# Causal masks written by TensorE under the logits, other banks and another order of work in an attention and FFN block

## The chip, the cores and the metric

One core of a Trainium2 chip. The metric is the device time of one execution in microseconds; three runs of the kernel before have a median of 406.66 us (405.45 to 406.77). TensorE multiplies, VectorE, ScalarE and GpSimd (POOL in the rows) do elementwise work, SyncE issues most DMAs. PSUM has eight banks, all in use.

## The reference

Eight sequences of 512 tokens with 128 channels pass through causal attention with 16 heads of 8 channels, a layernorm, a gated FFN on a time-shifted mixture, and a second layernorm:

```python
qkv = x @ w_attn + b_attn                      # x: (8, 512, 128)
att = softmax(where(causal, (q @ k.T) / sqrt(8), -inf))
y   = (att @ v) @ w_proj + b_proj
x1  = layernorm(x + y)
xr, xk = mu_r*x1 + (1-mu_r)*x1_prev, mu_k*x1 + (1-mu_k)*x1_prev
out = layernorm(x1 + sigmoid(xr @ W_r.T) * (square(relu(xk @ W_k.T)) @ W_v.T))
```

All is float32 at the borders. The kernel keeps q and k as sums of three bf16 parts (high, mid, low).

## The kernel before

A batch (one sequence) has 4 groups of 10 units, so 40 steps, and 8 batches make 320 steps. A unit is one 128x512 bank of logits at most: one half (side) of the array's rows, and one or two 64-row tiles of the triangle, as `EX_TILES` lists them; two heads stand in the two halves of the columns (`ab`). Every logit is computed twice. `maxima(m)` (L407 to L423) computes q·k into a bank of `mx_ps` for the row maxima: `reduce_maxima` (L681) on VectorE adds a mask and reduces with one instruction and an accumulator read for each tile. The maxima of a group are split into two bf16 parts by POOL (`parts`, L902), turned by VectorE (`maxima_turned`) and put by four DMAs of SyncE (`stack_maxima`, L304) into rows of `q_st`, where they act as one more term of the product. `logits(n)` (L425 to L440) then computes k·q minus the maximum, transposed, into a bank of `ex_ps`, ScalarE takes the exponential into `probs` (`exps`, L592), POOL sets the triangle behind the diagonal to zero with affine selects (`zero_behind`, L917; the waits of their users go through `squares_zeroed`), and `weighted_values` (L442 to L457) multiplies with the values in float32, which also gives the row sums.

Maxima run 20 steps ahead (`LEAD`), changed by `AHEAD` at some steps. Since there are two banks for logits, `logits(n)` waits until the exponential n-2 is done; the three maxima banks work likewise. In step 20 of a batch the maxima of the next batch begin, and these need the next batch's stacked q and k: xT is transposed (step 2), q (step 6) and k (step 7) are multiplied, ScalarE rounds the high part (`highs`, L597), VectorE takes the rest (`rests`, L705), ScalarE the mid part (`mids`, L603), POOL the low part (`lows`, L944), and SyncE copies each part into its bands of `q_st` or `k_st` with twelve DMAs of 128 KB (`stack`, L284, issue at L295), in one queue with `stack_maxima`, loads and stores.

Stage products (xT, q, k, v, proj, x1T, kT, r, kv) share two banks `sh_ps`, dealt in turn (`shared_uses`, L81). After the attention of a batch, during the next one, VectorE turns the sums (`sums_turned`, L713), divides (`normalise`, L718), turns again, adds the residual, takes statistics and aggregates (L737, L744); POOL forms rstd (`deviations`, L955); VectorE norms (`attention_normed`, L757); TensorE, ScalarE and POOL do the FFN.

Each engine has its queue, written out by hand: in step n every engine runs its step's unit and then the stage work that the tables `PE_AT`, `ACT_AT`, `DVE_AT`, `POOL_AT` put at that step (a number over 40 is a step of the next batch, a negative one a step of the batch before). All engines run in order, so a wait holds all that stands behind it. Before the loop stands a head for batch 0; behind it a tail that does the last batch's stages in halves.

## Time and profile before

| | |
|---|---|
| median of three runs | 406.66 us |
| the profiled execution | 407.86 us, span 406.1 us |
| busy: PE | 330.0 us, 81% |
| busy: DVE | 287.2 us, 71% |
| busy: ACT | 208.9 us, 51% |
| busy: POOL | 205.9 us, 51% |
| mean granted clock of TensorE | 0.812 |

### The profile page before, as it was taken

The page shows a single profiled execution, that of the slowest core. Times are in us where ns is not written, and L with a number is a line of the kernel's source. Part 1 is how long each engine was busy: PE and PEld are TensorE (multiplying, and loading weights), DVE is VectorE, ACT ScalarE, POOL GpSimd, SP SyncE. Part 2 cuts the span into 40 slices and gives each one's busy share as a digit, 9 for nine tenths or more (in the row PEclk, how much of TensorE's full clock was granted, in tenths as well). Part 3 has the DMA queues.
Part 4 walks back from the last instruction along what each step waited for, and adds up shares of the span by engine and source line. Part 5 has one row for each costly group of instructions (what it writes and reads, how often), then busy time and mean ns, then how long its engine had stood idle before and what let it go on. Part 6 is the DMA issues. An engine that isn't in the chain of part 4 may idle for free.

```text
span 406.1 us, 10267 instructions
## 1 busy us (share of the span) xinstructions
PE 330.0 (81%) x3721; PEld 153.5 (38%) x3721; DVE 287.2 (71%) x1326; ACT 208.9 (51%) x405; POOL 205.9 (51%) x404
## 2 busy tenths in 40 slices
PE   5268778987989698978998698979897989796853
PEld 2123323333443335333533335343534354424442
DVE  3379757788676887697778886887789778922254
ACT  3204655674565545583557546654667465544211
POOL 8131533453353933567454833593358545944642
PEclk9756758597979979796969888986999698669678
DMA  2611411041101410052102310141105100000000
GB/s 57 177 35 30 133 33 51 6 115 46 54 2 45 129 49 21 6 133 78 29 5 78 108 54 1 44 131 46 29 6 148 38 27 2 21 11 1 2 26 26
DMA packets 33114, 20.65 MB, mean 51 GB/s; under 512 B 7400, under 2 KB 33064, under 8 KB 33064
## 3 DMA queue, kind: packets, MB, share of 16 engines
q1 hardware_dynamic: 33064, 20.00, 18.3%
q8 instruction: 29, 0.48, 0.5%
q14 instruction: 21, 0.17, 0.1%
HBM read 4.72 MB, written 2.10 MB: 17 GB/s over the span
## 4 chain that ended last, share of the span: by engine, by line
PE 55%; DVE 16%; SPq 10%; ACT 5%; issue 5%; DMA 4%; POOL 4%; POOLq 0%; DVEq 0%; ACTq 0%
PE pv_ps L453 20%; PE ex_ps L437 12%; DVE masked L691 10%; SPq L295 7%; PE mx_ps L420 6%; ACT probs L592 5%; PE sh_ps L381 3%; SPq L304 3%; DMA q_st<-q_part 2%; PE sh_ps L494 2%; POOL probs L917 2%; PE sh_ps L391 2%; PE sh_ps L471 2%; PE sh_ps L463 2%; PE sh_ps L395 2%
## 5 line engine op out<-in xcount | busy, mean ns | idle before, releaser
L691 DVE CUSTOM_DVE_ANT_0 masked<-mx_ps,mask_wide 128x448 f32<-128x448 f32 (+7 forms) x512 | 204.9, 449 | 64.1 <-PE mx_ps L420 59.2
L592 ACT ACTIVATE probs<-ex_ps 128x512 f32<-128x512 f32 (+1 forms) x320 | 164.3, 553 | 145.1 <-PE ex_ps L437 142.7
L917 POOL TENSOR_SCALAR_AFFINE_SELECT probs<-probs 64x192 f32<-64x192 f32 (+2 forms) x212 | 94.9, 462 | 122.6 <-ACT probs L592 117.7
L420 PE MATMUL mx_ps<-k_st,q_st 64*64 64x128 bf16 (+7 forms) x1024 | 122.2, 346 | 29.2 <-DVE m_max L691 14.3
L437 PE MATMUL ex_ps<-q_st,k_st 64*64 64x64 bf16 (+7 forms) x1024 | 121.3, 340 | 21.9 <-ACT probs L592 18.9
L453 PE MATMUL pv_ps<-probs,vals 128*32 128x512 f32 (+7 forms) x1024 | 92.7, 489 | 0.0
L437 PEld LDWEIGHTS ex_ps<-q_st,k_st 64*64 64x64 bf16 x1024 | 44.4, 116 | 109.5 <-ACT probs L592 80.4
L420 PEld LDWEIGHTS mx_ps<-k_st,q_st 64*64 64x64 bf16 x1024 | 45.2, 117 | 55.1 <-DVE m_max L691 29.9
L691 DVE DVE_READ_ACCUMULATOR2_ANT m_max<- 128x1 f32 x512 | 42.5, 83 | 0.0
L453 PEld LDWEIGHTS pv_ps<-probs,vals 128*32 128x32 f32 x1024 | 26.4, 120 | 36.0 <-issue 27.5
L977 POOL TENSOR_SCALAR o_sb<-h,mv,rstd 128x128 f32<-128x128 f32 x28 | 22.1, 801 | 1.2 <-POOL rstd L960 1.1
L966 POOL TENSOR_TENSOR kact<-relu 128x512 f32<-128x512 f32 x7 | 7.3, 1039 | 20.2 <-ACT relu L627 15.8
L960 POOL TENSOR_TENSOR rstd<-var_eps,exponent 128x4 f32<-128x4 f32 x14 | 14.5, 1039 | 1.2
L737 DVE BATCH_NORM_STATS2 stats<-h 128x6 f32<-128x128 f32 x56 | 13.3, 281 | 2.2 <-POOL h L971 2.1
L761 DVE TENSOR_SCALAR x<-h,mv,rstd 128x128 f32<-128x128 f32 x28 | 7.9, 346 | 8.2 <-POOL rstd L960 8.2
L381 PE MATMUL sh_ps<-ident,x_in 128*128 128x128 f32 x32 | 7.8, 393 | 5.4 <-DMA x_in<-in_L_attn_x_dram 3.8
L716 DVE STREAM_TRANSPOSE y_rows<-pv_ps 128x512 f32<-128x512 f32 x15 | 10.7, 712 | 2.0 <-PE pv_ps L453 2.0
L907 POOL CAST m_part<-m_max 128x16 bf16<-128x16 f32 x32 | 6.3, 196 | 10.9 <-DVE m_max L691 9.0
L463 PE MATMUL sh_ps<-w_o,ynT 128*128 128x128 f32 x56 | 9.9, 332 | 2.2 <-DVE ynT L733 2.2
L494 PE MATMUL sh_ps<-w_mix,kact 128*128 128x128 f32 x56 | 10.8, 353 | 0.0
L476 PE MATMUL sh_ps<-w_mix,x1T 128*128 128x128 f32 x56 | 10.8, 275 | 0.0
L475 PE MATMUL sh_ps<-w_mix,x1T 128*128 128x128 f32 x56 | 10.8, 275 | 0.0
(126 smaller groups left out, 319.1 us busy)
## 6 DMA issues: line engine op xcount, KB each, us to landing
q_st<-q_part SPq DMA_DIRECT2D x48, 128.0 KB
k_st<-k_part SPq DMA_DIRECT2D x48, 128.0 KB, 2.4
x_in<-in_L_attn_x_dram SPq DMA_DIRECT2D x8, 256.0 KB, 2.8
q_st<-m_turn SPq DMA_DIRECT2D x128, 2.0 KB
x_res<-in_L_attn_x_dram SPq DMA_DIRECT2D x8, 256.0 KB, 2.7
out_dram<-o_sb SPq DMA_DIRECT2D x7, 256.0 KB, 2.3
q_st<-zero_b SPq DMA_DIRECT2D x8, 32.0 KB
out_dram<-o_sb SPq DMA_DIRECT2D x2, 128.0 KB, 1.8
```

The costliest lines, as they stand in the source:

```text
L295: sp.dma_start(st[band::BANDS, :, :], part_of[:, part, :]).then_inc(sem_of, 16)
L381: last = pe.transpose(ps[:, t * P:(t + 1) * P], src(t), ident[:, :])
L420: last = mm(ps[half_rows(ab), at:at + n], q_st[par][side_rows(s), slot, i * BLK:(i + 1) * BLK], k_st[par][side_rows(s), slot, 0:n], start= ...
L437: last = mm(ps[half_rows(ab), at:at + w], k_st[par][side_rows(s), slot, j * BLK:(j + 1) * BLK], q_st[par][side_rows(s), slot, j * BLK:T], ...
L453: last = mm(pv_ps[c * VW:(c + 1) * VW, j * BLK:T], vals[b % 2][:, 2 * c + h, j, :], probs[B % 2][:, gp, at:at + T - j * BLK], start=i == 0 ...
L463: last = mm(ps[:, t * P:(t + 1) * P], ynT[:, t * P:(t + 1) * P], w_o[:, :], start=True, stop=True)
L494: last = mm(ps[:, t * P:(t + 1) * P], kact[:, t * P:(t + 1) * P], w_mix[:, 4, :], start=True, stop=True)
L592: act.activation(probs[B % 2][:, gp, u * T:u * T + w], ex_bank(n)[0][:, 0:w], ACT.Exp, scale=SCALE).then_inc(exp_done, 1)
L691: last = dve.tensor_tensor_reduce(out=masked[m % len(masked)][:, at:at + n], in0=mx_ps[m % MX_BANKS][:, at:at + n], in1=mask_wide[:, T - n ...
L917: pool.affine_select(out=squares, in_=squares, compare_op=ALU.is_ge, fill=0.0, base=0, pattern=[[0, count], [1, BLK]], channel_multiplier= ...
L960: pool.tensor_tensor(rstd[i][:, :], var_eps[i][:, :], exponent[:, :], ALU.pow).then_inc(rstd_ready[i], 1)
L977: pool.tensor_scalar(o_sb[:, t, :], h2[:, t, :], mv[1][:, t, 0:1], rstd[1][:, t:t + 1], ALU.subtract, ALU.mult).then_inc(o_done, 1)
```

## The change

TensorE writes the masks: ahead of the logits of a unit, two matmuls of an identity (`ident_b`) with a triangle of large negative numbers (`behind_b`) go into the diagonal squares of the bank, and the logits are added to them. POOL's selects, `squares_zeroed` and the semaphore `causal` are gone; `weighted_values` waits for the exponentials. The tiles of a unit are in another order, so that both diagonal squares can be addressed by one pattern.

`ex_ps` has three banks and `sh_ps` one. For batch 0 each stage product has a bank of its own among banks not yet in use.

Small work is dealt out anew. ScalarE writes, besides the high part, a full copy of q and k (`q_full`, `k_full`), and POOL takes the rest from these two. POOL multiplies by the reciprocal sums (`normalise`), VectorE only takes the reciprocals (`shares`). The aggregates are gone for all batches but the last: POOL's `deviations` works from the statistics of even and odd columns with seven small operations in place of two, and gives a shift as well; ScalarE norms with scale and bias.

All tables are new, and a second set of them (`PE_END`, `ACT_END`, `DVE_END`, `POOL_END`, `PV_END`, `PV_LAST`) holds for stage work of the last batches. `AHEAD` now holds maxima back by one or two steps in steps 18 to 27.

In the head the weights and half of the bias go out on ScalarE's queue, and so do k's six stacking DMAs of batch 0; x is transposed in two halves that ScalarE and VectorE copy; VectorE takes the mid parts of batch 0; `b_v_wide` and its wait for the small vectors stand behind six maxima; and TensorE runs 5, 2 and 16 products of zeros (`idle_products`) between the head's work.

The diff, cut to its core:

```diff
-EX_TILES = ((0,), (1, 7), (2, 6), (3, 5), (4,))
+EX_TILES = ((0,), (7, 1), (6, 2), (5, 3), (4,))
-MX_BANKS, EX_BANKS = 3, 2
-AHEAD = {0: 0, 32: 1, 33: 1, 34: 3, 35: 3, 36: -1}
-PV_AT = {4: (0, 1), 6: (2, 3), 8: (4, 5), 10: (6, 7)}
-PE_AT = {"xT": -38, "q": -34, "k": -33, "v": -25, "proj": 59, "x1T": 69, "kT": 72, "r": 72, "kv": 78}
+MX_BANKS, EX_BANKS = 3, 3
+IDLE = (5, 2, 16)
+WT_AT = 8
+AHEAD = {2: 1, 8: 2, 9: 2, 13: 1, 18: -1, 19: -2, 20: -2, 21: -2, 22: -1, 23: -1, 24: -2, 25: -2, 26: -2, 27: -2,
+         36: 1, 37: 2, 38: 2, 39: -1}
+PV_AT = {0: (0,), 5: (1,), 7: (2, 3, 4), 8: (5,), 11: (6, 7)}
+PE_AT = {"xT": -40, "q": -37, "k": -35, "v": -25, "proj": 57, "x1T": 68, "kT": 74, "r": 76, "kv": 78}
+ACT_AT = {"xT": -40, "q": -37, "k": -35, "q_mid": -32, "k_mid": -31, "v": -25, "norm1": 67, "norm1b": 67, "x1T": 68,
+          "kT": 73, "r": 76}
+POOL_AT = {"q_rest": -35, "k_rest": -33, "q_low": -29, "k_low": -28, "yn0": 33, "yn1": 54, "residual": 6,
+           "deviations1": 64, "squares": 71, "add2": 81, "deviations2": 95, "norm2": 98}
+PE_END = {"proj": 59, "x1T": 70, "kT": 72, "r": 75, "kv": 77}
...
         ex_ps = [bank_of(f"ex_ps{i}") for i in range(EX_BANKS)]
-        sh_ps = [bank_of(f"sh_ps{i}") for i in range(2)]
+        sh_ps = bank_of("sh_ps")
+        head_ps = dict(zip(AHEAD_OF_ALL, (sh_ps, mx_ps[1], ex_ps[0], ex_ps[1], pv_ps, ex_ps[2], sh_ps)))
...
             sp.dma_start(x_in[0][:, :, :], x_d[0]).then_inc(xin_loaded[0], 16)
-            sp.dma_start(w_in[:, :], w_attn).then_inc(w_in_loaded, 16)
...
             for part in range(3):
-                for which in range(2):
-                    stack(which, part, 0)
+                stack(sp, 0, part, 0)
...
                 (ps, before), at = ex_bank(n), 0
                 wait(pe, exp_done, n - before + 1)
+                hidden = behind_b[side_rows(s), 0:2, :] if len(tiles) > 1 else behind_b[side_rows(s), 0, :]
+                for ab in range(2):
+                    mm(diagonals(ps, ab, T - tiles[0] * BLK, len(tiles)), ident_b[side_rows(s), :], hidden,
+                       start=True, stop=False, skip_group_check=True)
...
-                                  q_st[par][side_rows(s), slot, j * BLK:T], start=True, stop=True)
+                                  q_st[par][side_rows(s), slot, j * BLK:T], start=False, stop=True,
+                                  skip_group_check=True)
...
-                wait(pe, causal, squares_zeroed(2 * B + groups[-1], k, j))
+                wait(pe, exp_done, (2 * B + groups[-1]) * UNITS + SIDES * (k + 1))
...
+            def idle_products(n, bank_of_idle):
+                for _ in range(n):
+                    mm(bank_of_idle[:, :], idle[:, 0:P], idle[:, :], start=True, stop=True)
...
+            idle_products(IDLE[2], mx_ps[0])
             pe.wait_ge(ones_stacked[0], 16)
-            for m in range(MX_BANKS):
+            for m in range(WT_AT):
                 maxima(m)
...
                 act.activation(part[:, 0, :], ps[:, :], ACT.Identity, bias=bias[:, 0:1]).then_inc(high[i], 1)
+                if b > 0:
+                    act.activation(full[:, :], ps[:, :], ACT.Identity, bias=bias[:, 0:1]).then_inc(read, 1)
...
+            def attention_normed(b, tiles):
+                wait(act, h2_done, b)
+                wait(act, shift_ready[0], b + 1)
+                for t in tiles:
+                    act.activation(x1[:, t, :], h1[:, t, :], ACT.Identity, scale=rstd[0][:, t:t + 1],
+                                   bias=shift[0][:, t:t + 1]).then_inc(x1_done, 1)
...
+            act.dma_start(w_in[:, :], w_attn).then_inc(w_in_loaded, 16)
+            load_bias(act, 1, b_k)
...
+            for part in range(3):
+                stack(act, 1, part, 0)
...
+                if m == WT_AT - 2:
+                    dve.wait_ge(vecs_loaded, 64)
+                    dve.tensor_copy(b_v_wide[:, :], b_v[:, 0:1].to_broadcast([P, P])).then_inc(consts_v, 1)
...
-            def zero_behind(G, ab, first, apart, count):
...
-            def group_zeroed(G, second):
...
-            def unit_zeroed(G, k):
...
+            def rests(i, b):
+                full, part, rest = ((q_full, q_part, q_rest), (k_full, k_part, k_rest))[i]
+                wait(pool, high[i], b + 1)
+                wait_read(pool, ("q", "k")[i], b)
+                pool.tensor_tensor(rest[:, :], full[:, :], part[:, 0, :], ALU.subtract).then_inc(rested[i], 1)

```

## Rows read from the trace of the kernel before

**Rows 1.** Chain of waits of the page, share of the span by engine

```profile
PE 55%; DVE 16%; SPq 10%; ACT 5%; issue 5%; DMA 4%; POOL 4%; POOLq 0%; DVEq 0%; ACTq 0%
```

**Rows 2.** Windows: stretch, length, busy of PE, PEld, DVE, ACT, POOL; clock, DMA

```profile
35.07:73.93 38.86, 31.17 (x366) 12.52 (x362) 28.45 (x140) 24.22 (x47) 13.69 (x30) 0.68 0.22 58
...
73.93:337.57 263.64, 230.37 (x2788) 107.31 (x2784) 205.47 (x971) 154.40 (x300) 140.51 (x263) 0.86 0.21 55
...
295.13:337.57 42.44, 36.97 (x468) 17.67 (x468) 34.75 (x165) 25.62 (x51) 24.38 (x45) 0.89 0.20 53
337.57:379.71 42.14, 34.64 (x360) 15.98 (x364) 21.76 (x97) 22.04 (x43) 27.25 (x65) 0.78 0.03 9
```

**Rows 3.** Windows around the clock: before a fall, after it, and a full-speed stretch

```profile
93.00:96.40 3.40, 1.79 (x12) 1.18 (x12) 2.65 (x12) 1.28 (x3) 2.34 (x6) 1.00 0.30 78
96.40:103.30 6.90, 6.60 (x56) 2.08 (x59) 4.50 (x25) 2.17 (x4) 2.17 (x5) 0.51 0.11 24
...
280.80:314.90 34.10, 29.31 (x414) 14.88 (x406) 29.04 (x137) 22.75 (x45) 18.79 (x34) 1.00 0.21 57
```

**Rows 4.** TensorE's matmul waits, 73.93 to 337.57: total us, times, longest

```profile
PE ex_ps L437 <- ACT probs L592: 12.0, 32, 0.8
PE mx_ps L420 <- DVE m_max L691: 10.3, 18, 0.8
PE mx_ps L420 <- DMA q_st<-q_part: 4.3, 3, 1.6
```

**Rows 5.** Timeline of SyncE's queue and TensorE in batch 4: start, us, what [idle]

```profile
217.40 1.88 SPq L295 DMA_DIRECT2D q_st<-q_part  x3
...
227.15 0.58 SPq L295 DMA_DIRECT2D q_st<-q_part  x1
...
230.25 0.65 PE L420 MATMUL mx_ps<-k_st,q_st 64*64 64x512 bf16 x4 [1.55 <-DMA q_st<-q_part]
```

**Rows 6.** Groups by line, engine, tiles and form: busy us, mean ns, idle

```profile
L917 POOL TENSOR_SCALAR_AFFINE_SELECT probs<-probs 64x192 f32<-64x192 f32 (+2 forms) x212 | 94.9, 462 | 122.6 <-ACT probs L592 117.7
...
L947 POOL TENSOR_TENSOR q_part<-q_rest,q_part 128x512 bf16<-128x512 f32 x7 | 8.1, 1157 | 0.0
...
L761 DVE TENSOR_SCALAR x<-h,mv,rstd 128x128 f32<-128x128 f32 x28 | 7.9, 346 | 8.2 <-POOL rstd L960 8.2
...
L723 DVE TENSOR_TENSOR yn_rows<-y_rows,rden 128x256 f32<-128x256 f32 x15 | 6.4, 425 | 0.5
...
L710 DVE SCALAR_TENSOR_TENSOR q_rest<-sh_ps,b_q,q_part 128x512 f32<-128x512 f32 x8 | 6.0, 748 | 3.9 <-ACT q_part L601 3.9
...
L601 ACT ACTIVATE q_part<-sh_ps,b_q 128x512 bf16<-128x512 f32 x8 | 5.5, 683 | 2.3 <-PE sh_ps L391 2.3
```

**Rows 7.** Timeline of TensorE: matmuls of 64 and 128 columns, full, then half clock

```profile
221.28 0.19 PE L437 MATMUL ex_ps<-q_st,k_st 64*64 64x64 bf16 x2
221.74 0.22 PE L437 MATMUL ex_ps<-q_st,k_st 64*64 64x128 bf16 x2
...
47.50 0.32 PE L437 MATMUL ex_ps<-q_st,k_st 64*64 64x128 bf16 x2
```

**Rows 8.** Timelines: the head (four engines), then one stage product and its reader

```profile
15.66 0.61 SPq L295 DMA_DIRECT2D k_st<-k_part  x1
...
18.17 1.06 PE L420 MATMUL mx_ps<-k_st,q_st 64*64 64x512 bf16 x8 [6.83 <-DMA k_st<-k_part]
...
22.71 0.23 DVE L790 COPY b_v_wide<-b_v 128x128 f32<-128x128 f32 x1 [8.21 <-DMA mu<-in_L_ffn_mu_k_dram]
...
35.07 0.60 ACT L592 ACTIVATE probs<-ex_ps 128x512 f32<-128x512 f32 x1 [13.69 <-PE ex_ps L437]
...
214.69 1.13 PE L391 MATMUL sh_ps<-xT,w_q 128*128 128x512 f32 x2
...
216.69 0.68 ACT L601 ACTIVATE q_part<-sh_ps,b_q 128x512 bf16<-128x512 f32 x1
```

**Rows 9.** Timeline of VectorE near the end of batch 7

```profile
366.35 1.19 DVE L761 TENSOR_SCALAR x<-h,mv,rstd 128x128 f32<-128x128 f32 x4 [8.25 <-POOL rstd L960]
```

More of the change, by code:

```diff
@@ new lines, with due @@
+PV_LAST = {22: (0,), 23: (1, 2), 24: (3, 4, 5), 27: (6, 7)}
+TABLES = {"PE": (PE_AT, PE_END), "ACT": (ACT_AT, ACT_END), "DVE": (DVE_AT, DVE_END), "POOL": (POOL_AT, POOL_END)}
+GROUP_AT = {"parts": 1, "turn": 2}
+SHARED = tuple(PE_AT)
+AHEAD_OF_ALL = ("xT", "xT2", "q", "k", "v", "wT", "bp")
+def due(engine, name, n):
+    at, end = TABLES[engine]
+    last = NB - 2 if at[name] > STEPS else NB - 1
+    if name in end and n == last * STEPS + end[name]:
+        return last
+    s, rest = divmod(n - at[name], STEPS)
+    first, last = (0, last - 1) if name in end else (1, last)
@@ L96, in shared_uses @@
             if s is not None:
[L97 to L101 removed]
+                at[s, name] = len(at) + 1
+    return at
+SHARED_USES = shared_uses()
 def wait(eng, sem, value):
@@ L278, in in_bank, with load_bias, stack @@
             return slice(t * P % HALF, t * P % HALF + P)
+        def load_bias(eng, i, bias):
+            natural = b_attn[i * C:(i + 1) * C].rearrange("(s j d a) -> s d j a", s=SIDES, d=HD, a=1)
+            for s in range(SIDES):
+                eng.dma_start(bias[side_rows(s), :], natural[s],
+                              allow_slow_non_contiguous=True).then_inc(b_qk_loaded, 16)
+        def stack(eng, which, part, b):
+            par = b % 2
+            if part == 0:
+                wait(eng, exp_done, (b - 1) * STEPS)
+                if which == 0 and b > 0:
+                    eng.dma_start(q_st[par][MAX_BAND::MAX_STEP, :, :], zero_b[:, :]).then_inc(q_stacked, 16)
+            st, part_of, sem_of = ((q_st[par], q_part, q_stacked), (k_st[par], k_part, k_stacked))[which]
+            wait(eng, (high, mid, low)[part][which], b + 1)
+            for band, band_part in enumerate((Q_PARTS, K_PARTS)[which]):
+                if band_part == part:
+                    eng.dma_start(st[band::BANDS, :, :], part_of[:, part, :]).then_inc(sem_of, 16)
         block = ctx.enter_context(nc.Block())
@@ L781, in _ @@
                                 ).then_inc(consts_v, 1)
+            ps, read = wait_full(dve, "xT2", 0)
+            dve.tensor_copy(xT[:, HALF:T], ps[:, 0:HALF]).then_inc(read, 1)
             dve.wait_ge(b_qk_loaded, 64)
-            rests(0, 0)
-            rests(1, 0)
-            for i, (part, rest) in enumerate(((q_part, q_rest), (k_part, k_rest))):
-                dve.wait_ge(mid[i], 1)
-                dve.tensor_tensor(part[:, 2, :], rest[:, :], part[:, 1, :], ALU.subtract).then_inc(low[i], 1)
+            for i in range(2):
+                first_rests(i)
+                first_mids(i)
+            for i in range(2):
+                first_lows(i)
+            for half in range(2):
+                last = dve.tensor_copy(ident_b[half_rows(half), :], ident[half_rows(half), half * BLK:(half + 1) * BLK])
+            last.then_inc(consts_v, 1)
+            dve.wait_ge(mask_ready, 6)
+            dve.tensor_copy(behind_b[:, :, :], behind[:, :, :]).then_inc(consts_v, 1)
             dve.memset(q_st[1][:, :, :].bitcast(U32), 0).then_inc(consts_v, 1)
-            dve.wait_ge(vecs_loaded, 64)
-            dve.tensor_copy(b_v_wide[:, :], b_v[:, 0:1].to_broadcast([P, P])).then_inc(consts_v, 1)
-            dve.wait_ge(mask_ready, 3)
             for n in range(-LEAD, EXPS + BEHIND):
@@ L998, in _ @@
                 pool.wait_ge(mask_ready, 2 + ab)
+            pool.memset(behind[:, :, :], 0.0).then_inc(mask_ready, 1)
+            pool.wait_ge(mask_ready, 4)
+            for ab in range(2):
+                here = behind[half_rows(ab), :, :]
+                pool.affine_select(out=here, in_=here, compare_op=ALU.is_ge, fill=MASKED, base=0,
+                                   pattern=[[0, 2], [1, BLK]], channel_multiplier=-1).then_inc(mask_ready, 1)
+                pool.wait_ge(mask_ready, 5 + ab)
             pool.memset(vals[0][:, :, :, :], 0.0).then_inc(consts_g, 1)
```

399 lines of the change are left out of this document (204 added, 195 removed).

## The prediction

> **What bounds the kernel now.** I read the chain of waits first. Over half of the span passes on TensorE, a sixth on VectorE and a tenth in the queue of SyncE that issues the stacking transfers [rows 1]. So TensorE leads, and it is not alone. Next the stretches by batch: the profiled execution (span 406.13 us; 407.86 us as timed, against a median of 406.66 us) falls into a head of 35.1 us to the first exponential, batch 0 with 38.9 us, six regular batches with 263.6 us together, so 43.9 us each, batch 7 with 42.1 us, and the rest, 26.4 us [rows 2]. Of a regular batch TensorE is busy 38.4 us, VectorE 34.2, ScalarE 25.7, POOL 23.4 [rows 2]. TensorE's 38.4 busy us are not 38.4 us of full-speed work: the mean granted clock is 0.86 of full, which is about 33.0 us of work at 2.4 GHz. The period is therefore 33.0 us of work, 5.4 us lost to the clock, and 5.5 us idle.
>
> The third view is the clock around its falls. In the 3.4 us ahead of a fall TensorE was busy 1.79 us (waiting in the middle of a batch for the next batch's stacks), then it ran 6.9 us at 1.2 GHz; in the 34.1 us that passed wholly at 2.4 GHz it was busy 29.3 us [rows 3]. The Trainium skill (TensorE: Matmul & The Clock Gate, HAM oscillation) ties a return to half rate to long waits of TensorE; here its longest regular wait is about 1.6 us, and the clock falls all the same, so I go by the rows. The fourth view is what TensorE waits for in the six batches: ScalarE's release of one of two logits banks 12.0 us, VectorE's release of a maxima bank 10.3, the last part of q 4.3 [rows 4]. The weight-load row of the same answer is longer, but weight loads run beside matmuls, so I price from the matmul rows only. The fifth is the queue of SyncE: the first piece of q is issued at 217.4 us, the last at 227.15, and the maxima of the next batch start at 230.25 after a wait of 1.55 us [rows 5].
>
> **The change, part by part.**
>
> *POOL's zeroing goes.* 212 selects, 94.9 us in all, 11.9 us a batch [rows 6]. POOL is not the bound, so this pays only where somebody waited. In the regular batches that is nobody I can see in the matmul rows of [rows 4]; in the last one it is real, since the rstd of batch 6 stands behind selects that wait for exponentials, and VectorE sat idle 8.25 us for it, with TensorE behind [rows 9]. I take nothing from regular batches here and return to batch 7 below.
>
> *TensorE's triangles come.* Each of 320 steps gets two more 64-row matmuls of 64 or 128 columns ahead of the logits, on the same rows as the logits. The trace holds matmuls of this size in the same quarter of the array: one of 64 columns took 0.19 us and one of 128 took 0.22 at full clock, 0.32 at half [rows 7]. The constant part overlaps the next one, so the added time is the slope: 0.03 us for 64 columns, twice for 128, the two halves of the array side by side. A group has 4 steps of 64 and 6 of 128 columns: 4×0.03 + 6×0.06 = 0.48 us, 1.9 us a batch; with 10 per cent for issue, 2.1 us. Bounds: 0 if all of it lies in waits, and 80 whole durations of about 0.2, 16 us, if nothing overlapped; I stay at the slope since the rows of both forms show pairs starting together. The Trainium skill (same page, Back-to-back issue gap) puts an issue floor of about 25 ns under a small matmul; by it the 64-column ones would cost the same 0.03 us, and the sum would not move.
>
> *A third bank for logits, one for stages.* This takes aim at the 12.0 us of [rows 4], 2.0 us a batch. With three banks an exponential may end a step later before TensorE stands. ScalarE also gets more: one full copy each of q and k at up to 0.69 us, and four norms of 128 columns, at most half of that each, so up to 2.7 us a batch, bounded below by 1.5 when they start back to back. I take half, 1.0 us. The price is the single stage bank: nine uses a batch, each of which must be read before the next may be written. The rows show one such turn: q's product starts at 214.69, its reader runs at 216.69 for 0.68 [rows 8]. Now two reads stand there, and k's product waits for both. The tables put two to eleven steps between neighbours, so I add 0.5 us a batch, and make the dear case a rival.
>
> *VectorE's small work.* Off it go the rests of q and k (2×0.75), both products of normalise (2×0.43), four norms (1.13 a batch from 7.9 us in 7 batches), together 3.5 us, and eight small aggregates besides [rows 6]. That leaves some 30 us of 34.2. What TensorE waits for it, 10.3 us in six batches, is 1.7 a batch; I take 0.6 of that. Who waits on POOL for the same work: its rests are like the low parts, 1.16 us instead of 0.75 [rows 6], so the chain high, rest, mid, low grows by 0.8 us for the pair, and POOL has selects of 11.9 us less in its queue. The small operations of deviations go from two to seven; I bound them by nothing and by 0.4 us each and take 0.2, which lengthens the chain to the norm by 1 us; it has many steps of slack except in batch 7.
>
> *Preparation earlier, maxima later.* q's product moves from step 6 to 3 and k's from 7 to 5, and the first maxima of the next batch are let back by two steps. A step is about 1.1 us (43.9/40), so the queue of [rows 5] starts some 3 us earlier and its result is wanted 2 us later, against 1.55 us of wait and 0.8 of chain. That wait goes: 4.3 us by [rows 4] plus the start behind it, 1.0 us a batch. Issues on SyncE stay as many and in the same order, so nothing new is queued behind a wait there.
>
> *Sum of a regular batch.* Idle 5.5 − 1.0 (banks) + 0.5 (stage bank) − 0.6 (VectorE) − 1.0 (stacks) = 3.4 us. Work 33.0 + 2.1 = 35.1. With the clock at 0.86 that would be 40.8 + 3.4 = 44.2, nothing gained. But the clock fell behind lean stretches, and two of the edits fill these: no wait at the stacks, and more columns in each step. In the batch at 0.89 the period was 42.4, and that still with one slow stretch [rows 2]. I take one slow stretch less per batch, a clock of 0.95: 36.9 + 3.4 = 40.3. Gain 3.6 us, six times 21.6.
>
> *Head.* The last piece of k was issued at 15.66 and the first maxima ran from 18.17; then VectorE waited until 22.71 for vectors that it needs only for b_v_wide, and the first exponential came at 35.07 [rows 8], 12.3 us behind. Now that copy stands behind six maxima, and q and k go out on two queues. 12 issues of about 0.6 us in one queue [rows 5] become six and six; the last k is issued around 12.8, as the low parts are ready then, so maxima start at about 15.5, VectorE half a us later, and the first exponential at 16.1 + 12.1 = 28.2. Gain 6.9 us. Sixteen idle products stand ahead of the first maxima: at 2.4 GHz, 0.2 us each, they end in time; at half clock they end 2 us late. The Trainium skill (DMA: Bandwidth & Descriptors, Issuing engines are not separate DMA queues) calls what a second issuing engine saves usually small; by that the 2.7 us of it would be gone, and the head would gain 4.2.
>
> *Batch 0 and batch 7, rest.* Batch 0 has less on TensorE (31.2 us busy of 38.9) and VectorE, relieved by its share, is near its bound; with the wait for the stacks gone I take 2.5 us. Batch 7: the regular gain of 3.6 us and half of a VectorE wait that TensorE shared [rows 9] but which the longer deviations eat; 3.6 in all. The rest after the last exponential keeps its chain; without selects ahead of it 0.5 us.
>
> Total: 6.9 + 2.5 + 21.6 + 3.6 + 0.5 = 35.1, so a span of 371.0; with the 0.5 us by which the median lies over the span, 371.5.
>
> **Rivals.** *A, the clock holds all through.* The 34.1 us at full clock [rows 3] show that it can. Then 35.1 work and 14 per cent idle as in that row (4.8 of 34.1), less the 1.9 us of the edits: 35.1 + 5.7 − 1.9 = 38.9, a further 1.4 us in eight batches, and up to 2 us more in head and rest: 358. *B, the clock stays as it is.* Lean stretches come back at kT, r and kv, which remain. Then the regular batches give nothing (44.2), and head, batch 0 and rest give 9.9: 396. *C, slower: the single stage bank.* Each of nine products waits for the reader of the one before, at the head of TensorE's queue, with all logits and maxima behind it. My gains are 35 us over 63 such turns, so it decides from 35/63 = 0.56 us of wait per turn; the row of q shows 1.3 us from product to end of one reader [rows 8], and at 0.8 us a turn it costs 50 us: 421. Against it: the tables leave steps in between. *D, the triangles aren't hidden and cost like whole small matmuls* on the logits path, 0.2 us in 40 steps, 8 us a batch where I took 2.1: eight batches add 47 us to 371.5, 418; against it speak the pairs that start together.
>
> **Chances.** Forecast 0.60 (about 363 to 383), A 0.18, B 0.13, C 0.05, D 0.04. The likeliest is 371.5. The range takes in A with a few us below it, and leaves out C, D and most of B, 2 in 10 together: 353 to 391. A measurement tells about 0.3 per cent, 1.2 us, from no change. Faster 0.90, the same 0.02 (B with a worse head), slower 0.08.
>
> **What would show it.** First exponential at 28 us; nine turns without waits over 0.5 us on the stage bank; no TensorE wait for the last part of q; logits waits for ScalarE halved; granted clock in regular batches 0.95 and period 40.3; VectorE busy 30 us a batch. Wrong would be: a clock of 0.86 with a busier TensorE (B), stage products idle before (C), matmuls of the triangles with 0.1 us or more of their own (D).

## The result, and the profile after

The kernel after takes 335.69 us (333.71 to 336.87), the one before 406.06 (405.23 to 406.77), four runs each: a ratio of 0.826 [0.821, 0.831]. That is faster, as forecast, and by twice the forecast: 70 us in place of 35, below the whole range. Here and below every median takes in all executions, and the ratios leave out the few that came out in a slower state. The profiled execution of after has a span of 331.8 us and a mean granted clock of 0.950 (406.1 and 0.812 before).

The page of after: instructions busy, the granted clock in 40 slices (tenths), the chain of waits. To be read against the table of before and [rows 1].

```profile
PE 295.2 (89%) x4384; PEld 155.4 (47%) x4384; DVE 262.3 (79%) x1220; ACT 218.3 (66%) x445; POOL 145.0 (44%) x310
...
PEclk9965879899999999999999999999999999999958
...
PE 58%; DVE 13%; ACT 8%; POOL 7%; issue 6%; SPq 4%; DMA 2%; ACTq 0%; POOLq 0%; DVEq 0%
```

In the clock's line a 9 stands for 90 per cent of full speed or more. TensorE is now busy 89 per cent of the span; SyncE's queue, 10 per cent of the chain before, is 4. From the ninth slice (66 us) to the 38th the clock never falls. The stretches, with the same columns as [rows 2]: head, batch 0, the first regular batch alone, all six of them, batch 7, the rest.

```profile
0.00:32.36 32.36, 24.14 (x138) 9.55 (x138) 23.25 (x81) 4.71 (x7) 15.76 (x35) 0.79 0.41 93
32.36:65.02 32.66, 27.52 (x446) 14.30 (x448) 26.26 (x136) 24.51 (x49) 7.49 (x13) 0.87 0.26 69
65.02:101.15 36.13, 34.58 (x548) 17.96 (x544) 30.55 (x148) 27.41 (x57) 12.88 (x26) 0.98 0.24 63
65.02:276.31 211.29, 202.51 (x3268) 107.47 (x3264) 183.25 (x883) 164.13 (x337) 99.99 (x212) 1.00 0.26 69
276.31:307.69 31.38, 28.78 (x446) 14.99 (x442) 17.58 (x81) 22.61 (x48) 12.73 (x31) 1.00 0.04 11
307.69:331.80 24.11, 12.25 (x100) 9.11 (x92) 11.97 (x44) 2.31 (x6) 9.02 (x21) 0.81 0.07 22
```

A regular batch takes 211.29 / 6 = 35.2 us against 43.9. TensorE is busy 33.75 us of it (38.4 before) and idle 1.5 (5.5 before). The first figure is the clock's: the 5.4 us that it cost are gone, while the work at full speed rose by 0.7, from 33.0 to 33.7. So of the 8.7 us gained in a batch, 4.7 (5.4 − 0.7) come from the clock less the new work, and 4.0 from waits. What TensorE's matmuls still wait for there, to be read against [rows 4] (the same stretch of work, same columns):

```profile
PE sh_ps L514 <- ACT vals L690: 4.9, 6, 0.8
PE ex_ps L481 <- DMA q_st<-m_turn: 0.7, 2, 0.4
PE mx_ps L465 <- issue: 0.7, 1, 0.7
```

ScalarE's release of a logits bank (12.0 us), VectorE's of a maxima bank (10.3) and the last part of q (4.3) have all gone to nothing that shows. Left is one turn of the single stage bank in each batch, 0.8 us.

By stretch, the 74.3 us of the span came so (forecast behind it): head 2.7 (6.9), batch 0 6.2 (2.5), regular batches 52.4 (21.6), batch 7 10.8 (3.6), rest 2.3 (0.5).

### The profile page after: what moved, and what is told of

Read it like the earlier page. It is cut to its first block, busy times and chain, and to the rows that moved or that the text cites. A ratio compares the mean times of both kernels' runs of the same rounds, so it can differ in the third digit from the quotient of the medians.

```text
span 331.8 us, 11490 instructions
## 1 busy us (share of the span) xinstructions
PE 295.2 (89%) x4384; PEld 155.4 (47%) x4384; DVE 262.3 (79%) x1220; ACT 218.3 (66%) x445; POOL 145.0 (44%) x310
## 4 chain that ended last, share of the span: by engine, by line
PE 58%; DVE 13%; ACT 8%; POOL 7%; issue 6%; SPq 4%; DMA 2%; ACTq 0%; POOLq 0%; DVEq 0%
PE pv_ps L504 13%; DVE masked L781 8%; PE mx_ps L465 7%; PE ex_ps L487 7%; PE ex_ps L481 6%; ACT x L703 3%; SPq L337 3%; PE sh_ps L424 3%; PE sh_ps L434 2%; PE sh_ps L549 2%; PE sh_ps L526 2%; PE sh_ps L439 2%; PE sh_ps L522 2%; POOL rstd L1039 2%; PE sh_ps L527 2%
## 5 line engine op out<-in xcount | busy, mean ns | idle before, releaser
L665 ACT ACTIVATE probs<-ex_ps 128x512 f32<-128x512 f32 (+1 forms) x320 | 156.0, 560 | 36.9 <-PE ex_ps L487 36.0
L465 PE MATMUL mx_ps<-k_st,q_st 64*64 64x512 bf16 (+7 forms) x1024 | 104.8, 305 | 10.3 <-DMA k_st<-k_part 4.8
L487 PE MATMUL ex_ps<-q_st,k_st 64*64 64x512 bf16 (+7 forms) x1024 | 92.0, 289 | 0.0
L504 PE MATMUL pv_ps<-probs,vals 128*32 128x512 f32 (+7 forms) x1024 | 78.7, 417 | 0.0
L481 PE MATMUL ex_ps<-behind_b,ident_b 64*64 64x128 bf16 (+1 forms) x640 | 65.3, 222 | 3.5 <-ACT probs L665 2.5
L481 PEld LDWEIGHTS ex_ps<-behind_b,ident_b 64*64 64x64 bf16 x640 | 30.2, 105 | 61.9 <-ACT probs L665 40.6
L465 PEld LDWEIGHTS mx_ps<-k_st,q_st 64*64 64x64 bf16 x1024 | 43.9, 108 | 27.9 <-DVE m_max L781 18.0
L1013 POOL TENSOR_TENSOR yn_rows<-y_rows,rden 128x256 f32<-128x256 f32 x15 | 9.5, 631 | 28.9 <-DVE rden L821 28.9
L833 DVE BATCH_NORM_STATS2 stats<-h 128x6 f32<-128x128 f32 x56 | 13.4, 283 | 1.4 <-POOL h L1053 1.4
L703 ACT ACTIVATE x<-h,shift,rstd 128x128 f32<-128x128 f32 x28 | 11.5, 482 | 2.7 <-POOL shift L1041 2.6
L1059 POOL TENSOR_SCALAR o_sb<-h,rstd,shift 128x128 f32<-128x128 f32 x28 | 12.5, 459 | 1.0 <-POOL shift L1041 0.9
L526 PE MATMUL sh_ps<-w_mix,x1T 128*128 128x128 f32 x56 | 11.5, 287 | 0.1
(161 smaller groups left out, 362.9 us busy)
```

The source lines that it names most:

```text
L465: last = mm(ps[half_rows(ab), at:at + n], q_st[par][side_rows(s), slot, i * BLK:(i + 1) * BLK], k_st[par][side_rows(s), slot, 0:n], start= ...
L481: mm(diagonals(ps, ab, T - tiles[0] * BLK, len(tiles)), ident_b[side_rows(s), :], hidden, start=True, stop=False, skip_group_check=True)
L487: last = mm(ps[half_rows(ab), at:at + w], k_st[par][side_rows(s), slot, j * BLK:(j + 1) * BLK], q_st[par][side_rows(s), slot, j * BLK:T], ...
L504: last = mm(pv_ps[c * VW:(c + 1) * VW, j * BLK:T], vals[b % 2][:, 2 * c + h, j, :], probs[B % 2][:, gp, at:at + T - j * BLK], start=i == 0 ...
L526: mm(ps, x1T[:, 1 + t * P:1 + (t + 1) * P], w_mix[:, 2, :], start=True, stop=False)
L665: act.activation(probs[B % 2][:, gp, u * T:u * T + w], ex_bank(n)[0][:, 0:w], ACT.Exp, scale=SCALE).then_inc(exp_done, 1)
```

## The experiments

The theories after the result were these. *Filler*: the triangles' matmuls keep TensorE from lean stretches, and the clock with it. *Bank*: the third logits bank alone takes most of the waits, and the clock follows. *POOL*: the selects, which I had at nothing, stand in somebody's way. *Order*: the tables do it, and each removal only makes room for them. Every run is given as the ratio to before on its own chip with its 95 per cent interval; "worth" means the difference in ratio to after's 0.826, times 406 us. The clock is the mean of the profiled execution. The kernel after was not run again beside these runs, and three kernels that differ little from it (after_noidle, after_late_memset, after_v) all came out at 0.836 or 0.837. So a worth is uncertain by some 4 us, and differences of 1 per cent are not read.

| run | median us | ratio | clock |
|---|---|---|---|
| before_filler | 407.3 | 1.005 [1.000, 1.009] | 0.848 |
| before_tri | 402.5 | 0.996 [0.992, 1.000] | 0.843 |
| after_notri | 334.9 | 0.829 [0.826, 0.831] | 0.935 |
| after_2ex | 367.9 | 0.910 [0.908, 0.913] | 0.940 |
| after_zeroing | 405.6 | 1.003 [1.000, 1.006] | 0.854 |
| after_dve | 344.4 | 0.855 [0.845, 0.865] | 0.956 |
| after_noahead | 361.3 | 0.886 [0.874, 0.899] | 0.889 |
| after_noidle | 338.5 | 0.837 [0.830, 0.843] | 0.931 |
| after_poolload | 381.8 | 0.947 [0.941, 0.952] | 0.906 |
| after_zeroing_late | 390.7 | 0.969 [0.963, 0.975] | 0.886 |
| after_late_memset | 336.7 | 0.837 [0.830, 0.843] | 0.949 |
| after_v | 340.2 | 0.836 [0.828, 0.844] | 0.935 |
| after_poolload_nowait | 362.9 | 0.893 [0.886, 0.901] | 0.926 |
| after_zeroing_2ex | 430.0 | 1.058 [1.050, 1.066] | 0.837 |

### Do more matmuls hold the clock, and what do the triangles cost?

before_filler puts two small matmuls ahead of each unit's logits in the kernel before; the logits overwrite them.

```diff
                 wait(pe, exp_done, n - before + 1)
+                w = BLK * len(tiles)
+                for ab in range(2):
+                    mm(ps[half_rows(ab), 0:w], k_st[par][side_rows(s), slot_of(g, ab), 0:BLK],
+                       q_st[par][side_rows(s), slot_of(g, ab), 0:w], start=True, stop=True)
```

> The kernel before, with two more small matmuls of 64 or 128 columns into the logits bank ahead of each unit's logits, which then overwrite them; nothing else is changed. Theory 1 (the added matmuls fill TensorE's lean stretches and so hold the clock): mean granted clock 0.93 or more, time 385 to 395 us. Theory 2 (the clock follows from order, banks and a lighter VectorE, the matmuls are a plain cost): clock stays 0.80 to 0.85, time 408 to 425 us.

before_tri gives the kernel before the real triangles and takes POOL's selects out; banks, tables and small work stay.

```diff
+                for ab in range(2):
+                    mm(diagonals(ps, ab, T - tiles[0] * BLK, len(tiles)), ident_b[side_rows(s), :], hidden,
+                       start=True, stop=False, skip_group_check=True)
...
-                wait(pe, causal, squares_zeroed(2 * B + groups[-1], k, j))
+                wait(pe, exp_done, (2 * B + groups[-1]) * UNITS + SIDES * (k + 1))
...
-                        group_zeroed(G, second)
```

> The kernel before, with this one part of the change alone: TensorE writes the triangles, POOL zeroes nothing, banks, tables and all else stay. Theory 1: clock 0.93 or more, 380 to 392 us. Theory 2: 400 to 415 us, clock near 0.82; the selects gone are worth no more than 5 us, mostly at the end.

after_notri leaves the triangles out of after, so that nothing masks.

```diff
-                    mm(diagonals(ps, ab, T - tiles[0] * BLK, len(tiles)), ident_b[side_rows(s), :], hidden,
-                       start=True, stop=False, skip_group_check=True)
```

> The changed kernel without the triangle matmuls and without any mask, so what lies behind the diagonal is not hidden. Theory 1: the clock falls to half in each batch again, 345 us or more. Theory 2: the clock stays full from batch 1 on, and the time falls by the cost of the matmuls, 1.0 to 1.9 us a batch: 320 to 328 us.

Windows over the six regular batches of before_filler, of before_tri and of after_notri, in this order (columns as in [rows 2]):

```profile
74.02:334.04 260.02, 228.41 (x3266) 117.70 (x3264) 205.50 (x972) 154.65 (x300) 140.54 (x263) 0.89 0.21 56
```

```profile
73.35:333.59 260.24, 229.22 (x3266) 117.48 (x3264) 204.36 (x972) 154.40 (x301) 73.02 (x119) 0.88 0.20 56
```

```profile
66.21:275.68 209.47, 198.80 (x2788) 98.29 (x2789) 183.30 (x885) 163.79 (x337) 99.65 (x212) 0.99 0.26 69
```

With the filler the granted clock of the regular batches is a little higher, 0.89 against 0.86, and the time comes out half a per cent longer: the theory of the filler fell. The triangles are nearly free: after does 33.7 us of full-speed work a batch, after_notri 198.80 / 6 × 0.99 = 32.8, and the two times lie within 1 us of each other. Neither theory for after_notri held: without triangles the clock did not fall in each batch (0.99), and the time did not come down to 320 to 328 us either. Most telling is before_tri. POOL is relieved of half of its work (140.5 us busy to 73.0), nobody waits for a select, and yet only 0.4 per cent comes of it, with an interval that reaches no change. For the old order my term "nothing from regular batches" was right to within 0.6 us a batch (260.24 us for six in place of 263.64). That holds although in the kernel before something did wait for the selects there: not a matmul, but weight loads.

```profile
PEld pv_ps L453 <- POOL probs L917: 5.4, 14, 0.7
```

### What is the third bank worth?

```diff
-            return ex_ps[n % EX_BANKS], EX_BANKS
+            return ex_ps[n % 2], 2
```

> The changed kernel with two of its three logits banks in use. If the third bank carries the fall in idle time (1.3 us a batch against 5.5), the waits for ScalarE's release come back at 2 us a batch or more, the clock falls in places, 350 to 365 us. If it is the order of the stages that carries it: 336 to 342 us.

The five regular batches at the end, and what TensorE waited for in them:

```profile
110.74:307.41 196.67, 172.60 (x2724) 87.73 (x2720) 155.19 (x736) 140.78 (x281) 86.75 (x186) 1.00 0.23 63
```

```profile
PE ex_ps L481 <- ACT probs L665: 18.0, 45, 0.8
PE sh_ps L514 <- ACT vals L690: 4.1, 5, 0.8
```

The period is 196.67 / 5 = 39.3 us, 4.1 more than after, and 18.0 / 5 = 3.6 of them are this one wait. In the whole kernel the bank is worth 34 us, where I had 1.0 a batch. But it does not bring the clock: with two banks and 24.1 of 196.67 us idle (12 per cent, as much as before) the clock stayed at 1.00, where I had expected it to fall in places. So the bank theory holds for the waits and falls for the clock.

### Is POOL's zeroing in the way of the new order?

after_zeroing puts before's selects, their semaphore and the waits for it into after, in place of the triangles. All else of the change stays.

```diff
-                wait(pe, exp_done, (2 * B + groups[-1]) * UNITS + SIDES * (k + 1))
+                wait(pe, causal, squares_zeroed(2 * B + groups[-1], k, j))
...
-GROUP_AT = {"parts": 1, "turn": 2}
+GROUP_AT = {"zero0": 8, "zero1": 11, "parts": 1, "turn": 2}
...
+                        group_zeroed(G, second)
```

> The changed kernel with the mask done as before: POOL zeroes behind the diagonal with its affine selects and the values wait for that; no triangle matmuls. All else as changed. If the selects were only work beside the path (as the prediction has it): POOL rises by 11.9 us a batch to about 29 of 35, and the time stays at 333 to 340 us. If the tight schedule can't carry them (POOL's rests, low parts and products of the sums queue behind selects that wait for exponentials): 345 to 375 us.

The whole of the gain is gone: 405.6 us, more than either theory had. First the window of five regular batches, then TensorE's waits and one of VectorE's over the whole kernel:

```profile
117.96:339.92 221.96, 180.69 (x2320) 85.93 (x2320) 152.64 (x736) 135.69 (x282) 143.45 (x305) 0.88 0.21 55
```

```profile
PE pv_ps L507 <- POOL probs L1000: 34.7, 22, 3.4
PE mx_ps L473 <- DVE m_max L784: 16.2, 26, 1.6
PE sh_ps L517 <- DVE ynT L831: 10.3, 7, 1.6
...
DVE m_turn L795 <- POOL m_part L992: 21.7, 14, 1.9
```

The period is 221.96 / 5 = 44.4 us, 8.3 of it idle, and the clock is back at 0.88. With before, after and before_tri this makes a square, and it is the central finding:

| | order, banks and small work of before | of after |
|---|---|---|
| POOL's selects | 1 | 1.003 [1.000, 1.006] |
| TensorE's triangles | 0.996 [0.992, 1.000] | 0.826 [0.821, 0.831] |

Neither half brings anything alone; together they bring 17 per cent. The second half is a bundle, order, banks, small work and head together. The rows above say how the selects hold the new kernel up, and three runs take it apart.

after_poolload keeps the triangles, so nobody waits for a select, but POOL does as many selects of the same size on a tile of its own (scratch), at the same places and behind the same waits for exponentials. after_poolload_nowait takes those waits out of POOL's queue as well. In the cut below the added lines are of both, the removed one is what sets the second apart from the first.

```diff
+                rows = scratch[half_rows(ab), 0:count * width]
+                pool.affine_select(out=squares, in_=squares, compare_op=ALU.is_ge, fill=0.0, base=0,
+                                   pattern=[[0, count], [1, BLK]], channel_multiplier=-1).then_inc(causal, 1)
...
-                    wait(pool, exp_done, (G + 1) * UNITS)
```

> The changed kernel, TensorE still writing the triangles, with POOL's selects added on a scratch tile: as many, as large, at the same places of its queue and with the same waits for exponentials, but nobody waits for them. Theory 3 (POOL's in-order queue: selects that wait for exponentials hold up the rests, low parts, products and rstd behind them): most of the 70 us of the kernel with zeroing come back, 370 to 400 us. Theory 4 (the direct wait of the values' matmuls for the selects, at the early places where the new tables put them): 338 to 350 us.

> As the run with POOL's selects on a scratch tile, but they don't wait for exponentials either: the same work in POOL's queue, no wait of its own. Theory 3a (POOL stands in its queue waiting for exponentials, and parts, rests and products stand behind it): 338 to 350 us. Theory 3b (the 11.9 us a batch of work itself is too much for POOL's place in the chain): 365 us or more.

after_zeroing_late is after_zeroing with before's later steps for the product with the values.

```diff
-PV_AT = {0: (0,), 5: (1,), 7: (2, 3, 4), 8: (5,), 11: (6, 7)}
+PV_AT = {4: (0, 1), 6: (2, 3), 8: (4, 5), 10: (6, 7)}
```

> The changed kernel with POOL's zeroing in place of the triangles, as in the run that took 405.6 us, and with the values' matmuls at the steps they had before (4, 6, 8, 10 in place of 0, 5, 7, 8, 11). Theory 4 (direct wait at early places): the 34.7 us of TensorE's waits for selects mostly go, 345 to 375 us. Theory 3 (POOL's queue): 385 us or more.

The longest waits of POOL, VectorE and TensorE in after_poolload:

```profile
POOL scratch L1000 <- ACT probs L669: 46.3, 30, 4.0
...
DVE m_turn L796 <- POOL m_part L993: 25.9, 21, 1.9
...
PE mx_ps L469 <- DVE m_max L785: 19.5, 31, 1.5
```

and in after_poolload_nowait, TensorE's, VectorE's and one of ScalarE's:

```profile
PE sh_ps L428 <- ACT x L707: 13.9, 7, 2.2
PE sh_ps L518 <- DVE ynT L832: 10.9, 7, 1.6
...
DVE ynT L832 <- POOL yn_rows L1045: 9.7, 7, 1.4
...
ACT x L707 <- POOL shift L1073: 18.3, 7, 3.1
```

So the 72 us that the selects cost in the new kernel have three parts, as the runs add them one by one. POOL's time alone is 27 us: the norm's shift and the normalised rows, both now POOL's, come late, ScalarE and VectorE wait for them, and TensorE stands at a stage product in each batch (at most 2.2 and 1.6 us; 13.9 + 10.9 us in all). The waits for exponentials in POOL's queue add 22: POOL stands up to 4.0 us, `parts` stands behind it, VectorE turns the maxima late and then frees its maxima banks late. That others wait for the selects, above all TensorE at the values' product, adds 23: in after_zeroing its longest wait is 3.4 us. With the product at before's steps 14 us come back (ratio 0.969), and the wait falls from 34.7 to 13.2 us, while the wait for VectorE's maxima rises from 16.2 to 22.0. So the steps of the values' product are 14 of the 72 us; most of the rest passes through POOL's queue. after_poolload_nowait came between its two theories, the waits alone (338 to 350) and the work alone (365 or more), so both parts are real. The first is rather too large: the selects on scratch hold POOL some 7 us longer in the whole kernel than the real ones, since more of them wait for the one before.

```profile
PE mx_ps L473 <- DVE m_max L784: 22.0, 42, 1.1
PE pv_ps L507 <- POOL probs L1000: 13.2, 9, 2.6
```

after_zeroing_2ex undoes selects and third bank together:

```diff
-            return ex_ps[n % EX_BANKS], EX_BANKS
+            return ex_ps[n % 2], 2
```

> The changed kernel with POOL's zeroing in place of the triangles and with two logits banks. The third bank is worth 32 us with the triangles in place. If the two gains add: 405 + 32 = 437 us. If each is only worth something once the other bound is gone (TensorE then waits for POOL, not for banks): 405 to 415 us.

It is the slowest kernel of all, 1.058: the change with these two parts undone loses to the kernel before. From there the bank alone brings 22 us and the triangles alone 60 (1.058 to 0.910), 82 together; both at once bring 94. So the two gains nearly add, and help each other by 12 us.

### Small work, held-back maxima, idle products, the values' step

after_dve gives rests, normalise's product and the norm back to VectorE (no full copies on ScalarE; POOL keeps the seven small operations).

```diff
-                if (b := due("POOL", "yn0", n)) is not None:
-                    normalise(b * BATCHES)
...
+                for i, name in enumerate(("q", "k")):
+                    if (b := due("DVE", f"{name}_rest", n)) is not None:
+                        later_rests(i, b)
...
+                for half, name in enumerate(("norm1", "norm1b")):
+                    if (b := due("DVE", name, n)) is not None:
+                        attention_normed(b, (2 * half, 2 * half + 1))
```

> The changed kernel with the small work back on VectorE: the rests of q and k, the products of normalise and the four norms, as before; aggregates stay away. VectorE gets back 3.5 us a batch, ScalarE loses 2.7, POOL 3.5. If VectorE's load carries the gain (34 of 35 us busy would make it the bound): 350 us or more. If it was slack: 334 to 341 us.

after_noahead takes the steps by which maxima run ahead or are held back:

```diff
-AHEAD = {2: 1, 8: 2, 9: 2, 13: 1, 18: -1, 19: -2, 20: -2, 21: -2, 22: -1, 23: -1, 24: -2, 25: -2, 26: -2, 27: -2,
-         36: 1, 37: 2, 38: 2, 39: -1}
+AHEAD = {}
```

> The changed kernel with maxima always 20 steps ahead, neither held back nor let forward. If holding them back keeps TensorE from the wait for the next batch's stacks: a wait of 1 to 3 us a batch for the parts of q or k comes back, with a fall of the clock behind it, 345 to 360 us. If the earlier preparation alone does it: 335 to 340 us.

The small work is worth 12 us, give or take 5 by the two intervals. VectorE is busy 168.05 / 5 = 33.6 us a batch in after_dve against 30.5, the period 36.6 against 35.2, and the clock stays full. TensorE now waits for VectorE's norm and rests in each of these five batches:

```profile
100.62:283.84 183.22, 169.14 (x2724) 89.44 (x2720) 168.05 (x776) 123.66 (x252) 71.35 (x165) 1.00 0.25 67
```

```profile
PE sh_ps L424 <- DVE x L836: 3.7, 5, 0.7
PE sh_ps L439 <- DVE q_rest L829: 3.4, 5, 0.7
```

The table of held-back maxima is worth 24 us, give or take 5. Its profiled execution took 365.7 us where the median is 361.3, so I read only which wait is there; it is the wait for the stacks that I had named in the kernel before, each about as long:

```profile
PE mx_ps L464 <- DMA q_st<-q_part: 8.5, 6, 1.6
```

These 8.5 us in six waits are a third of the 24. What the rest is (the clock, or the maxima's place in the other steps) stays open.

after_noidle takes out the idle products, and after_v puts the values' product and its reader two steps earlier, by one number in each of two tables:

```diff
-IDLE = (5, 2, 16)
+IDLE = (0, 0, 0)
```

> The changed kernel without its 23 idle products in the head. If they are worth something: q and k of batch 0 run at half clock and the first exponential comes 1 to 2 us later. If not (the first maxima wait for a DMA until 18.67 us in any case, and the clock has fallen by then): first exponential and time within 1 us of the changed kernel.

```diff
-PE_AT = {"xT": -40, "q": -37, "k": -35, "v": -25, "proj": 57, "x1T": 68, "kT": 74, "r": 76, "kv": 78}
+PE_AT = {"xT": -40, "q": -37, "k": -35, "v": -27, "proj": 57, "x1T": 68, "kT": 74, "r": 76, "kv": 78}
```

> The changed kernel with the values of a batch computed and read two steps earlier (step 13 in place of 15), so that proj in step 17 finds the one stage bank read: its wait of 0.8 us a batch, 4.9 us in all, goes. If nothing takes its place: 330 to 332 us. If the product of the next stage or the maxima are late next: 335 to 337 us.

Neither can be told from after with certainty (0.837 and 0.836, intervals that overlap after's), and neither is faster. Without idle products the first exponential comes at 32.41 us in place of 32.36: they don't shorten the head. Moving v frees the stage bank earlier and takes the 4.9 us wait away, but another comes in the place of it, 8.1 us in the whole kernel, where after has 2.5. So a wait of 4.9 us, taken away, was worth nothing:

```profile
PE ex_ps L481 <- ACT probs L665: 8.1, 11, 1.1
```

### Why the head gave 2.7 us and not 6.9

The head of after, SyncE's and ScalarE's queues, two of VectorE's casts, POOL's two fills, the first maxima and the first exponential (columns as in [rows 5]):

```profile
9.13 1.81 POOL L1091 MEMSET k_st<- 128x2048 uint32 x1
9.46 4.94 SPq L337 DMA_DIRECT2D q_st<-q_part  x5
9.69 1.54 DVE L805 CAST q_part<-q_rest 128x512 bf16<-128x512 f32 x1
10.03 5.29 ACTq L337 DMA_DIRECT2D k_st<-k_part  x6
10.89 2.08 POOL L1092 MEMSET vals<- 128x2048 f32 x1
11.91 1.33 DVE L805 CAST k_part<-k_rest 128x512 bf16<-128x512 f32 x1
...
13.76 0.68 DVE L810 TENSOR_TENSOR k_part<-k_rest,k_part 128x512 bf16<-128x512 f32 x1
...
18.67 0.94 PE L465 MATMUL mx_ps<-k_st,q_st 64*64 64x512 bf16 x8 [4.81 <-DMA k_st<-k_part]
...
32.36 0.60 ACT L665 ACTIVATE probs<-ex_ps 128x512 f32<-128x512 f32 x1 [7.71 <-PE ex_ps L487]
```

The maxima start at 18.67 us, later than before's 18.17 [rows 8]. Two things were in doubt: the casts beside POOL's zeros, and the transfers. after_late_memset moves the zeros behind the low parts.

```diff
+            pool.wait_ge(low[1], 1)
             pool.memset(k_st[1][:, :, :].bitcast(U32), 0).then_inc(consts_g, 1)
```

> The changed kernel with POOL's memsets of the second k_st and vals held until the low part of k is done. In the changed kernel VectorE's two casts of the mid parts took 1.54 and 1.33 us while POOL filled these tiles. If the two engines get in each other's way: casts of about 0.7 us or less, and the first exponential 1 to 2 us earlier, 334 us. If a cast costs that by itself: casts as before, time as before.

Its casts and the pair that now stands beside the zeros:

```profile
9.77 0.43 DVE L805 CAST q_part<-q_rest 128x512 bf16<-128x512 f32 x1
10.89 0.43 DVE L805 CAST k_part<-k_rest 128x512 bf16<-128x512 f32 x1
12.44 2.06 DVE L874 CAST ident_b<-ident 64x64 bf16<-64x64 f32 x2
```

The casts run in 0.43 us in place of 1.54 and 1.33, and the maxima still start at 18.54 us, the first exponential at 32.29. So the casts weren't the limit. What probably was shows in the DMA share (the last but one column), first of after, then of before in its stretch ahead of the maxima:

```profile
12.00:18.60 6.60, 1.86 (x9) 0.66 (x7) 4.73 (x7) 1.18 (x2) 1.76 (x7) 1.00 1.11 221
```

```profile
12.00:18.00 6.00, 0.00 (x0) 0.00 (x0) 2.12 (x2) 0.71 (x2) 0.12 (x2) 0.71 0.72 201
```

With two queues the last issue of k comes at 14.51 us in place of 15.66, right behind the low part that it copies (13.76 + 0.68 = 14.44). But the pieces take 2.8 to 4.0 us to land where before's took 2.3 to 2.6, at a share of 1.11 against 0.72 and nearly the same rate (221 and 201 GB/s). In after_late_memset the last issue comes another 1.1 us earlier, at 13.4, and the pieces take up to 5.1 us, so the maxima start at the same time. That fits DMA engines that are full. SyncE's queue, rid of k, also starts four weight loads of 64 KB from 14.44 on, which before began at 16.31; how much of the longer landing is theirs isn't shown, and no run undid the second queue alone. The Trainium skill (DMA: Bandwidth & Descriptors, Issuing engines are not separate DMA queues), which the prediction weighed, says just this: a second issuing engine saves sequencer time only. This trace agrees as far as it goes: the maxima did not start earlier.

## Why the prediction was right and wrong

*Right.* Faster; TensorE is the bound, and in regular batches all three waits of [rows 4] went. The stage bank was cheap: 4.9 us in 54 turns, 0.09 a turn against the 0.56 from which rival C decides, in one place only. VectorE busy 183.25 / 6 = 30.5 us a batch (30 said). B fell with the clock, and D, which had 8 us a batch for triangles that took 0.9. In the old order removing the selects alone gave next to nothing, as said.

*By the sum of a regular batch*, 40.3 us forecast and 35.2 measured, the miss of 5.1 has three terms: idle time 3.4 against 1.5, full-speed work 35.1 against 33.7 (1.4), and a clock of 0.95 against 1.00 (1.8). Six such batches are 31 of the 39 us by which the gain was forecast too small. The three steps below stand behind them.

*"I take nothing from regular batches here."* This is the step that failed, and the largest. It prices the removal in the kernel before, which has room for the selects. The change takes that room: it puts the product with the values at steps 0 to 11 in place of 4 to 10, and gives POOL the rests, the products of normalise and the seven small operations. There the selects cost 72 us. I read "no matmul waits for it" as "worth nothing", and I counted the gains of bank, order and small work as if they came with the selects in place or without; the runs show that with the selects in place all of them together come to nothing (after_zeroing, 1.003). This size could not be read from the matmul waits of before; what could be read is that POOL's selects wait 117.7 us for exponentials [rows 6], and that whatever else is in that queue waits with them.

*"I take half, 1.0 us"* for the third bank: it measured 4.1 a batch. The wait of [rows 4], 2.0 a batch, was no ceiling: with the other waits gone and two banks left, this one is 3.6 (after_2ex). Of VectorE's release (10.3 us) I took a third, and all of it went.

*The clock.* 0.95 forecast for regular batches, 1.00 measured, so rival A was the nearest; it gave 358 because it kept 14 per cent idle from the full-speed stretch of [rows 3], where 4 per cent was left. My reason, that more columns fill lean stretches, fell with before_filler: more columns in each step left the clock at 0.89. What did hold it is open. The six regular batches of the kernels whose waits are compared here:

| | idle share of TensorE | longest matmul wait, us | clock |
|---|---|---|---|
| before | 0.13 | 1.6 | 0.86 |
| before_filler | 0.12 | 1.6 | 0.89 |
| before_tri | 0.12 | 1.6 | 0.88 |
| after | 0.04 | 0.8 | 1.00 |
| after_dve | 0.08 | 0.7 | 1.00 |
| after_2ex | 0.12 | 0.8 | 0.99 |
| after_poolload_nowait | 0.12 | 2.2 | 0.98 |
| after_poolload | 0.14 | 2.2 | 0.94 |
| after_zeroing_late | 0.17 | 2.6 | 0.92 |
| after_zeroing | 0.19 | 3.4 | 0.87 |
| after_zeroing_2ex | 0.20 | 3.2 | 0.86 |

Neither column orders the clocks. Five kernels idle 12 or 13 per cent and have clocks from 0.86 to 0.99; and a longest wait of 2.2 us stands beside 0.98, one of 1.6 beside 0.86. Among the kernels with the new order alone the clock is by and large the lower the more TensorE idles. No run changed the waits and nothing else, so a cause isn't shown.

*Triangles*: 2.1 us a batch forecast, 0.9 of work measured, and no more than 1 us of time in the whole kernel. *Head*: 6.9 forecast, 2.7 measured; of the 2.7 us by which the second queue was to start the maxima earlier nothing came, they started 0.5 us later; and the path from the first maxima to the first exponential took 13.7 us where I had 12.7 (16.9 before), at half clock by the third and fourth of the 40 slices. What is left is that shorter path less a start 0.5 us later: 3.2 − 0.5 = 2.7. *Batch 0 and 7*: 2.5 and 3.6 forecast, 6.2 and 10.8 measured. In batch 7 the busy time fell by 5.9 us as the clock went from 0.78 to 1.00, and the idle time by 4.9; in batch 0 by 3.7 (0.68 to 0.87) and 2.5. I had given batch 0 nothing from the clock, and batch 7 only a regular batch's share.

*The range* was too narrow below since all terms were priced one by one against the old order. They are not independent: undone singly, selects (72), bank (34), held-back maxima (24) and small work (12) come to 142 us, twice the 70 of the whole. The selects alone cost 72 us in the new kernel, and were worth 0.4 per cent in the old one.

*Open.* How much the tables alone are worth. No run put the new tables without the banks onto the kernel before, nor the other way round. And whether the new kernel could carry the selects if the small work stood on VectorE again: no run undid selects and small work together, so of the 27 us of POOL's time it isn't shown how much is the tables' and how much the moved work's.

## What to carry to other kernels

An engine that nobody waits for can still be what the schedule was drawn around: when a change removes its work and also redraws the order, price the removal under the new order, or state that term as unknown with an upper bound far above zero. A wait in a profile bounds what its cause is worth from neither side when other things change with it: 2.0 us of wait a batch before stood for a bank worth 4.1, and 4.9 us of wait in after stood for nothing, as another wait took its place (after_v). To find out which half of a double change pays, build all four corners; here both halves alone gave nothing.

## What the runs showed of the hardware

A cast of 128x512 on VectorE took 0.43 us alone and 1.54 or 1.33 us beside POOL's memset, ending some 0.3 us behind it (11.23 against 10.94 and 13.24 against 12.97); in after_late_memset, where POOL's fills come later, the second of the two 64x64 casts took 1.87 us, against 0.19 in after. The Trainium skill (SBUF — State Buffer, SBUF: two separate sides) describes such a lock between the two engines, held for a whole instruction, and the trace agrees with it. A plan of a head has to reckon with POOL's zeros making a cast three times as long, though here that cost nothing.

POOL's norm of the output was 801 ns as subtract and multiply, and 459 ns as multiply and add, for the same 128x128 (before, then after). VectorE's norm did not change with the same swap, 346 and 343 ns (before, after_dve). No run parts the two operations from the columns that they read:

```profile
L977 POOL TENSOR_SCALAR o_sb<-h,mv,rstd 128x128 f32<-128x128 f32 x28 | 22.1, 801 | 1.2 <-POOL rstd L960 1.1
```

```profile
L1059 POOL TENSOR_SCALAR o_sb<-h,rstd,shift 128x128 f32<-128x128 f32 x28 | 12.5, 459 | 1.0 <-POOL shift L1041 0.9
```

And POOL's small operations of 128x4 cost the 0.2 us that I had taken for them:

```profile
L1023 POOL TENSOR_TENSOR apart<-stats 128x4 f32<-128x4 f32 x14 | 2.9, 207 | 7.3 <-DVE stats L833 7.3
```
